# Two scan tiles of a selective state space layer in one VectorE operation, on one Trainium2 core

## What is computed

```python
dt = softplus(proj[..., -1:] * W_dt[:, 0] + b_dt)      # 256 inner channels d
A = -exp(A_log)                                        # 256 channels x 16 states n
def step(h, inp):
    dt_t, Bt, Ct, xt = inp
    dA = exp(dt_t[..., None] * A)
    h = dA * h + (xt * dt_t)[..., None] * Bt[:, None, :]
    y = einsum('bdn,bn->bd', h, Ct)
    return h, y
_, ys = lax.scan(step, h0, inputs)
y = (ys + x_ssm * D_param) * silu(z)
x = layernorm(x + y @ W_out.T)
h = silu(w1(x)) * w2(x); h = gelu(h1(h)); h = gelu(h2(h))
x = layernorm(x + w3(h))
```

## Time and profile before

| what | value |
|---|---|
| time, median of 3 runs | 1031.45 us (1031.44 to 1032.19) |
| the profiled execution's own time | 1031.52 us |
| span of the profile (first to last instruction) | 1029.7 us |
| mean granted TensorE clock | 0.969 |

### The profile page before, as it was taken

One profiled execution on the slowest core, in us unless ns is written; L12 is line 12 of the kernel. 1 busy time (PEld: TensorE's weight loads), 2 busy tenths in 40 slices (PEclk: granted clock), 3 DMA queues, 4 the chain that ended last, 5 costly groups with the idle time before them and its releaser, 6 DMA issues.

```text
span 1029.7 us, 13659 instructions
## 1 busy us (share of the span) xinstructions
PE 965.2 (94%) x3852; PEld 427.8 (42%) x3852; DVE 935.2 (91%) x1115; ACT 897.1 (87%) x1500; POOL 881.5 (86%) x531
## 2 busy tenths in 40 slices
PE   5955899999999999999999999999999999999998
PEld 2312335353443435344443535344443535334454
DVE  2898999999999999999999999999999999999500
ACT  4397799999999999999999999999999999997242
POOL 3479998999999898999989898999989899988420
PEclk8586899999999999999999999999999999999999
DMA  5949488593939678593949669392948759393000
GB/s 190 264 156 273 115 227 203 154 271 100 279 95 266 164 215 227 128 272 102 283 103 261 178 188 254 109 282 88 278 130 232 208 157 259 98 276 85 0 11 10
DMA packets 110716, 185.16 MB, mean 180 GB/s; under 512 B 12976, under 2 KB 23728, under 8 KB 110640
## 3 DMA queue, kind: packets, MB, share of 16 engines
q1 hardware_dynamic: 110112, 183.98, 67.6%
q10 hardware_dynamic: 528, 0.32, 0.1%
HBM read 162.23 MB, written 22.02 MB: 179 GB/s over the span
## 4 chain that ended last, share of the span: by engine, by line
issue 34%; DVE 32%; ACT 16%; PE 12%; POOL 5%; DMA 0%; DVEq 0%; ACTq 0%; POOLq 0%; SPq 0%
DVE hb L853 17%; DVE U L842 12%; ACT dA L508 7%; PE GY L937 5%; POOL pb L403 3%; ACT L508 2%; ACT L616 2%; ACT hid L616 1%; ACT X L518 1%; PE GY L884 1%; PE GY L993 1%; PE GY L969 1%; DVE x L803 1%; PE GY L928 1%; DVE conv L787 1%
## 5 line engine op out<-in xcount | busy, mean ns | idle before, releaser
L403 POOL TENSOR_TENSOR pb<-hb,crep 128x1024 f32<-128x1024 f32 x256 | 602.6, 2366 | 48.7 <-DVE hb L853 35.9
L853 DVE TENSOR_TENSOR_SCAN hb<-dA,U 128x512 f32<-128x512 f32 x512 | 593.5, 1199 | 0.0
L842 DVE TENSOR_TENSOR U<-X,xdr 128x512 f32<-128x512 f32 x500 | 319.1, 684 | 8.4 <-ACT X L518 6.5
L508 ACT ACTIVATE dA<-dtr,negA 128x510 f32<-128x510 f32 x500 | 322.8, 714 | 3.7 <-DVE hb L853 3.2
L937 PE MATMUL GY<-g,h_sb 128*128 128x512 f32 x512 | 234.2, 601 | 0.0
L937 PE MATMUL GY<-hid,h_sb 128*128 128x512 f32 x512 | 228.3, 599 | 0.9 <-ACT g L757 0.7
L928 PE MATMUL GY<-pb,sel_sb 128*32 128x512 f32 x1024 | 139.9, 619 | 13.2 <-POOL pb L403 13.2
L937 PEld LDWEIGHTS GY<-g,h_sb 128*128 128x128 f32 x512 | 93.5, 190 | 138.2 <-issue 138.2
L937 PEld LDWEIGHTS GY<-hid,h_sb 128*128 128x128 f32 x512 | 93.9, 190 | 135.7 <-issue 125.6
L465 POOL TENSOR_TENSOR hid<-hid,g 128x512 f32<-128x512 f32 x64 | 80.9, 1277 | 9.6 <-ACT g L757 9.1
L941 PE MATMUL GY<-x1T,w_sb 128*128 128x512 f32 x128 | 69.3, 623 | 0.0
(11 more groups left out here) (130 smaller groups left out, 1052.7 us busy)
## 6 DMA issues: line engine op xcount, KB each, us to landing
dtr<-scr_dt SPq DMA_DIRECT2D x252, 256.0 KB, 8.1
xdr<-scr_xd SPq DMA_DIRECT2D x252, 256.0 KB, 7.4
brep<-scr_rows SPq DMA_DIRECT2D x32, 256.0 KB, 6.4
crep<-scr_rows SPq DMA_DIRECT2D x32, 256.0 KB, 8.9
scr_dt<-dts SPq DMA_DIRECT2D x32, 256.0 KB, 4.4
scr_xd<-xds SPq DMA_DIRECT2D x32, 256.0 KB, 4.6
xres<-xT_d SPq DMA_DIRECT2D x16, 256.0 KB, 9.3
xT_sb<-xT_d SPq DMA_DIRECT2D x15, 256.0 KB, 3.5
```

What stands on the lines that cost most here:

```text
L403: nc.gpsimd.tensor_tensor(pb[:, qs:qs + 2, :], hb[:, hs:hs + 2, :], crep[:, b % 2, g:g + 1, :].to_broadcast([P, 2, TB]), ALU.mult).then_in ...
L508: nc.scalar.activation(halves(dA[:, decay_slot(b, u), :])[:, :, 1:SEQ], halves(BREP[q] if by_product(b, k) else dtr[:, slot, q, :])[:, :, ...
L842: nc.vector.tensor_tensor(U[i][:], X[:], xdr[:, slot, q + i, :], ALU.mult).then_inc(s_u, 1)
L853: nc.vector.tensor_tensor_scan(hb[:, 2 * (v % H_PAIRS) + i, :], dA[:, decay_slot(j, u), :], U[i][:], 0.0, ALU.mult, ALU.add).then_inc(s_h, 1)
```

## The change

The two PSUM banks of U become one tensor of two banks. Except in the by_product groups, the two products of a pair are one operation over 1024 columns, with X read twice by a broadcast. The two scans of a pair are one operation over the flattened 1024 columns; the zeros in dA at columns 0, 256, 512 and 768 separate the four sequences. The counts of the semaphores stay the same (an operation over two tiles adds 2). The products of a pair wait once, for both scans of the pair before, and the scan waits for both decays and both products.

```diff
--- before.py
+++ after.py
@@ -130,7 +130,7 @@
         scr_dt = nc.dram_tensor("scr_dt", [2, NC, GT, PARITIES, SD, TB], F32, kind="Internal").ap()
         scr_xd = nc.dram_tensor("scr_xd", [2, NC, GT, PARITIES, SD, TB], F32, kind="Internal").ap()
 
-        U = [ps(f"U{i}", [P, TB]) for i in range(2)]
+        U = ps("U", [P, 2, TB])
         X = ps("X", [P, TB])
 
         GY = ps("GY", [P, 3 + NC, TB])
@@ -186,7 +186,7 @@
 
 
         G0, G1, G2, Y0, Y1 = G + Y
-        BROWS0, BDT0 = U[1][:], U[0][:]
+        BROWS0, BDT0 = U[:, 1, :], U[:, 0, :]
 
         BREP = (G0, G1, G2, Y1)
         BROWS, BDT = G1, G2
@@ -200,7 +200,7 @@
         BH1_2 = (GY[:, 0:2, :], GY[:, 2:4, :])
         BH2_2 = (GY[:, 1:3, :], GY[:, 0:2, :])
 
-        BLAST = (U[0][:], U[1][:], X[:], Y0)
+        BLAST = (U[:, 0, :], U[:, 1, :], X[:], Y0)
 
         def bank_in(b):
             return G0 if b < 2 else Y0
@@ -830,28 +830,29 @@
                             dve.wait_ge(s_X, 2)
                         elif v in (0, 4, 12):
                             dve.wait_ge(s_X, 3 * j + 1 + (0, 4, 12).index(v))
-                        for i in range(2):
-                            if v > 0 or j > 0:
-                                dve.wait_ge(s_h, TILES * j + 2 * v + i - 1)
-                            if by_product(j, k):
+                        if v > 0 or j > 0:
+                            dve.wait_ge(s_h, TILES * j + 2 * v)
+                        if by_product(j, k):
+                            for i in range(2):
                                 dve.wait_ge(s_rxd, 2 * v + i + 1)
-                                nc.vector.tensor_tensor(U[i][:], BREP[q + i], brep[:, states_of(k), :], ALU.mult).then_inc(s_u, 1)
-                            else:
-                                if fresh:
+                                nc.vector.tensor_tensor(U[:, i, :], BREP[q + i], brep[:, states_of(k), :], ALU.mult).then_inc(s_u, 1)
+                        else:
+                            if fresh:
+                                for i in range(2):
                                     dve.wait_ge(s_xdr[slot][q + i], 16 * loads_up_to(j, k, XD_SLOTS))
-                                nc.vector.tensor_tensor(U[i][:], X[:], xdr[:, slot, q + i, :], ALU.mult).then_inc(s_u, 1)
+                            nc.vector.tensor_tensor(U[:], X[:].unsqueeze(1).to_broadcast([P, 2, TB]), xdr[:, slot, q:q + 2, :],
+                                                    ALU.mult).then_inc(s_u, 2)
                         if v == 9 and tail:
                             scaled(yo, BW3, rs2, s_rs2, 2 * T + 2).then_inc(s_yo, 1)
                         if v == 10:
                             gate(j, 0)
                         if v >= H_PAIRS or j > 0:
                             dve.wait_ge(s_p, STEPS * j + v - H_PAIRS + 1)
-                        for i in range(2):
-                            u = 2 * v + i
-                            dve.wait_ge(s_dA, TILES * j + u + 1)
-                            dve.wait_ge(s_u, TILES * j + u + 1)
-                            nc.vector.tensor_tensor_scan(hb[:, 2 * (v % H_PAIRS) + i, :], dA[:, decay_slot(j, u), :], U[i][:],
-                                                         0.0, ALU.mult, ALU.add).then_inc(s_h, 1)
+                        dve.wait_ge(s_dA, TILES * j + 2 * v + 2)
+                        dve.wait_ge(s_u, TILES * j + 2 * v + 2)
+                        hs, ds = 2 * (v % H_PAIRS), decay_slot(j, 2 * v)
+                        nc.vector.tensor_tensor_scan(flat(hb[:, hs:hs + 2, :]), flat(dA[:, ds:ds + 2, :]), flat(U[:]),
+                                                     0.0, ALU.mult, ALU.add).then_inc(s_h, 2)
                     if v == 4 and j == 0:
                         taps(1)
                     if v == (0 if tail else 1) and front and j > 0:
```

## The result

The changed kernel takes 1089.51 us (median of 4 runs, 1086.85 to 1090.49) against 1031.45 us before: a ratio of 1.0551, 95% interval 1.0533 to 1.0569, so 58 us slower. The forecast was 1076.5 us (1047 to 1096), slower. The profiled execution took 1088.68 us (span 1086.9), 57.2 us more than the one of before.

What follows compares the result with a forecast made beforehand. VectorE's own stream was taken to bound each round. Dependent boundaries +78.9 us, saved instructions -27.2, vanished waits for X -6.7: +45.0 on 1031.52 gives 1076.5 us, range 1047 to 1096.

Steps and rivals of the forecast that it cites:

- The saving: VectorE's stream: two instructions fewer per pair at 0.06 us each, 0.12 us per pair, 227 pairs, -27.2 us.
- The price of a dependence: VectorE waiting for its direct neighbour: lost overlap 0.105 plus gap 0.10, 0.205 us at each of 385 boundaries, +78.9 us.
- The gap: From one VectorE instruction's end to its dependent neighbour's start: 0.10 us, read from round 0's taps; range 0.03 to 0.15.
- the signal now counts two at once ...; both I cost at nothing: At dependent boundaries: the semaphore count of two, and a fresh product's two load waits behind the scan wait, cost nothing.
- two ends of an unknown: Gap rows on VectorE: 0.10 us between round 0's taps, the value taken; 0.03 between two instructions of the start.
- the cover at the end: Round 15: 11 pairs slip 3.2 us into the 4.2 us before PE takes the last pb; costed at nothing.
- the cover held: Start: 12 pairs slip 3.5 us into VectorE's 4.12 us wait for POOL at 98.72; costed at nothing.
- A: Rival, VectorE's boundaries: the dependence is cheap, gap 0.03 us, +18 us, 1050 us; chance 0.14.
- B: Rival, VectorE: waiting for the neighbour costs nothing extra, 27 us go until ACT binds, about 1012 us; chance 0.09.
- C: Rival: no measurable change, a boundary costing just 0.09 us by chance; chance 0.03.
- D: Rival, PE: longer waits for x1 lower its clock each round and reach VectorE, 23 us more, 1100 us; chance 0.08.
- The wait for X: Products waiting for ACT's X, 6.5 us in all: with longer rounds some 11 such waits vanish, -6.7 us.

Runs made afterwards that it cites:

- n_both: Kernel before, operations narrow, with the changed kernel's waits: first product waits for both previous scans, first scan for both products; 1102.46 us (1.0672).
- bench: VectorE's products and scans alone: narrow with the waits as before, 3.42 us a pair; wide, each waiting for its neighbour, 3.73.
- bench2: VectorE's products and scans alone, seven stretches of 12 pairs, varying narrow or wide operations, order, broadcast and the count added to the semaphore.
- bench2 a: VectorE alone, wide operations with four banks of U, order product, product, scan, scan, no instruction waiting for its neighbour: 3.31 us a pair.
- bench2, e against f: VectorE alone, wide product without a broadcast, wide scan: e adds 2 to its semaphore, gap 0.09 to 0.10 us; f adds 1, gap 0.03.
- inc1: Changed kernel, but each wide operation adds 1 to its semaphore instead of 2, and all who wait count operations; 1075.88 us (1.0423).
- n_scan: Kernel before with one edit: the first scan of a pair waits for both products, so for its direct neighbour; 1070.03 us (1.0362).
- bench3: VectorE alone, seven stretches of 12 wide pairs, each instruction waiting for its neighbour, varying count added and met waits ahead or behind; 3.59 to 3.79 us a pair.
- bench3 c: VectorE alone, wide pairs, each instruction adds 1 and has two long met waits ahead of the one for its neighbour; 3.79 us a pair.
- inc1_order: Changed kernel with wide operations adding 1, and the scan's wait for its product placed ahead of those for POOL and decays; 1056.14 us (1.0228).
- n_coarse: Kernel before with the changed kernel's coarser signals to and from ACT, no dependence between neighbours on VectorE; 1032.37 us (1.0007).
- n_prod: Kernel before with one edit: the first product of a pair waits for both scans of the pair before; 1052.71 us (1.0197).
- w_scan: Changed kernel with the wide scan kept and the product as two narrow operations again; 1091.52 us (1.0581).
- bench2, c and d: VectorE alone: c, wide product, narrow scans, gap 0.04 us before scan, 0.11 before product; d, narrow products, wide scan, 0.11 before scan, 0.03 before product.

## Why the prediction was right, and by how much it was short

**What bounds the kernel, and the cause.** Right. VectorE's stream sets the round, and n_both shows that the two waits alone make the loss. The rule of the Trainium skill weighed there (the page "VectorE: DVE Perf Modes", section "The DRAIN you can't avoid", that a semaphore between chained operations costs nothing extra) did not hold here: bench has 3.42 us a pair without and 3.73 with two dependences, and fewer instructions.

**The saving.** 0.12 us per pair was predicted, 0.11 measured (3.42 to 3.31, bench2 a). The marginal cost of 512 elements holds as well: product 1.23 us, scan 2.29 us.

**The price of a dependence.** The lost overlap (0.105) holds: 3.31 + 2 x 0.105 + 0.10 + 0.13 = 3.75, the measured pair. The gap is the term that was mis-sized: it was put at 0.10 for both places, from the taps.

In front of the product 0.10 is what came, in part by luck. The step "the signal now counts two at once ...; both I cost at nothing" was wrong for the count: it costs 0.07 us (bench2, e against f), and without it the gap here is 0.03 (inc1). The taps count 1 and have their 0.10 from a met wait ahead of the one for the neighbour. The sum had the price of the count in it without knowing. For the load waits the step held: the products that have them behind the wait for the scan come 0.09 us after it. Only where a wait for X stands ahead it is more, 0.13 us, or 0.19 at v = 0.

In front of the scan it was 0.13, and that is a term that the sum lacks. The scan's waits for POOL and for its decays, long met, stand ahead of the one for its product, and two of them make 0.13 with a count of 1 (n_scan, inc1, bench3 c) as with 2. Nothing shows them as a releaser, and they still cost. The earlier trace rows and the earlier trace rows, which the prediction took as two ends of an unknown, are explained by the order: 0.10 has the wait for the neighbour last, 0.03 has it first. Some 200 scans at 0.03 us more are 6 us of the 13 us by which the forecast was short; most of the rest is 2.0 us at the start, 1.4 us of a new wait and 1 us of short holes, all told below, and 0.13 us a round in front of the products, whose mean gap is 0.11.

**Where it is paid.** By the taps of each round in the two profiled executions: up to round 1 +2.0 us (98.72 to 100.69; predicted 0), round 1 +6.0 (53.76 to 59.71, with 1.4 us of new wait for PE in front of its gate), the 12 rounds from 2 to 13 +44.3 (3.69 each, 3.2 predicted), from there to x1 of round 15 +5.3, and the rest -0.2: PE's chain from x1 to the end took 102.2 us before and 102.0 after. So the cover at the end was right to the tenth. At the start VectorE was ready 5.7 us later (3.5 predicted), and its 4.12 us wait for POOL shrank to 0.40: the cover held. Of the 2.0 us, 1.7 are there before the first product (25.92 us before, 27.59 after), ahead of anything that was changed. That start scatters from run to run, from 25.36 in n_coarse to 28.13 in n_prod, so they are chance and no cost of the change.

**The rivals.** A (gap 0.03) is what inc1_order reaches, 1056 us where A gave 1050, but not this change. B and C fell. D, the clock, was half right. PE's wait for x1 grew to 2.32 us (2.5 predicted) in all 12 steady rounds, and in six of them the granted clock fell behind it to 1.2 GHz for a part of the round (0.97 as the mean of the round, 1.00 in the others); timeline of PE in the round of 62.46 us (beside the earlier trace rows):

```profile
612.06 0.96 PE L989 MATMUL GY<-ident,x 128*128 128x128 f32 x4 [2.32 <-DVE x L803]
...
613.66 4.70 PE L970 MATMUL GY<-w_sb,hid 128*128 128x128 f32 x32
```

The 32 matmuls took 4.70 us instead of 3.74, in other rounds up to 5.37. But none of it is seen to reach VectorE. Of the six rounds with the fall, three are as long as those without, such as the one of 62.11 us in the table above (clock 0.97 too). The other three are 0.35 us longer by one hole each in VectorE's stream, 1 us in all, and the same hole is in rounds without a fall: in w_scan a round with the mean clock 1.00 took 62.69 us, its neighbour with 0.97 took 62.34. Timeline of that hole in w_scan:

```profile
698.08 1.30 DVE L844 TENSOR_TENSOR U<-X,xdr 128x512 f32<-128x512 f32 x2
699.86 2.29 DVE L854 TENSOR_TENSOR_SCAN hb<-dA,U 128x1024 f32<-128x1024 f32 x1 [0.48 <-DVE U L844]
```

So the holes aren't the clock's; what makes them stays open. The wait for X went as predicted, from 6.5 us to 0.7 us.

## What to carry to other kernels

Before two operations are merged, look at what the narrow ones wait for. If they form a stream in which each needs the one two before it, their fixed cost is already hidden to 0.06 us each, and merging can win no more than that; if the merged ones need their direct neighbour, each place costs 0.14 to 0.24 us. Merge only with a second buffer, so that the order can stay product, product, scan, scan. Where a dependence on the neighbour can't be avoided, let the instruction add 1 to one semaphore and state the wait that ends last first, the long met ones behind it: in this kernel these two edits, which change no work, gave back 33 of 58 us.

## What the runs showed of the hardware that was not expected

The gap from the end of a VectorE instruction to the start of the one that waits for it: 0.03 to 0.04 us with a single wait and a count of 1, also with one met wait behind it; 0.10 to 0.11 with a count of 2, or with one met wait ahead; 0.13 to 0.14 with two ahead, or with a count of 2 and one ahead; 0.09 with a count of 2 and one behind (bench2 and bench3). The count that matters is the one that the waiting instruction itself adds, not that of its neighbour (bench2, c and d). Without a dependence neither costs anything (bench2, a).

The timelines leave out what stands in these gaps, but the traces have it: a wait can be a record of its own, an EVENT_SEMAPHORE on DVEq, listed under the kernel's line of the wait. Lines of bench2 (the product of c, the scan of d, product and scan of e), and of the changed kernel (the scan's waits for its product and for POOL in one record); the numbers are count, then ns min/median/max:

```profile
L149 DVEq EVENT_SEMAPHORE  x12: 21/21/21, 91.4 to 132.1; - x12
L159 DVEq EVENT_SEMAPHORE  x12: 21/21/21, 137.1 to 178.1; - x12
L163 DVEq EVENT_SEMAPHORE  x12: 21/21/21, 180.5 to 221.4; - x12
L165 DVEq EVENT_SEMAPHORE  x12: 21/21/21, 181.8 to 222.8; - x12
...
L852 DVEq EVENT_SEMAPHORE  x256: 49/50/50, 28.9 to 1024.3; - x128
```

The waits of c's scan (L151), of d's product (L156) and both of f (L169, L171) have no such record. So an instruction that adds 1 carries one wait itself, and one that adds 2 carries none: its wait becomes a record ahead of it. In e this record starts 0.04 us after the neighbour's end and lasts 0.02, and the instruction starts 0.04 after it, 0.10 together. The wait that an instruction carries is the one written first; those behind it go into records, up to two in one. A record of two lasts 0.05 us where one lasts 0.02, and that is the step from 0.10 to 0.13 (the changed kernel, inc1). This is why the order of the waits matters: in inc1_order the scan carries the wait for its product, and the record with the other two is through before the product ends. Why the compiled program splits the waits so, the traces don't show.
